# Gated delta rule kernel: the products kept with a minus sign, the inverse's first transposed level copied from SBUF

## The reference, cut to what matters

```python
g = jnp.cumsum(g.reshape(Bq, H, NC, CHUNK), axis=-1)
decay = jnp.where(tril, jnp.exp(g[..., :, None] - g[..., None, :]), 0.0)
M = jnp.where(stril, jnp.einsum('bhncd,bhnmd->bhncm', k_beta, k) * decay, 0.0)
T = jax.scipy.linalg.solve_triangular(eye + M, jnp.broadcast_to(eye, M.shape), lower=True)
v_c = jnp.einsum('bhnij,bhnjd->bhnid', T, v_beta)
k_cumdecay = jnp.einsum('bhnij,bhnjd->bhnid', T, k_beta * jnp.exp(g)[..., None])
```

## Time and profile before

| | |
|---|---|
| median of 3 runs | 1333.41 us (1332.9 to 1334.39) |
| profiled execution, its own time | 1335.4 us |
| its span in the trace | 1333.6 us |
| PE busy | 1217.2 us |
| DVE busy | 1037.8 us |
| ACT busy | 903.4 us |
| POOL busy | 756.3 us |
| granted TensorE clock, mean | 0.985 |

### The profile page before, as it was taken

How to read it: one execution, slowest core, us unless ns; L and a number is a source line. 1 busy time by engine, 2 the same in 40 slices (tenths; PEclk the granted TensorE clock), 3 DMA queues, 4 the chain that set the end, 5 groups by cost and what they waited for, 6 DMA issues and landing times.

```text
span 1333.6 us, 32082 instructions
## 1 busy us (share of the span) xinstructions
PE 1217.2 (91%) x11612; PEld 863.4 (65%) x11612; DVE 1037.8 (78%) x1641; ACT 903.4 (68%) x1715; POOL 756.3 (57%) x792
## 2 busy tenths in 40 slices
PE   3678999999999999999999999999977589999997
PEld 2346676767767676767667676767665356666664
DVE  5586979888797979888897979798865676666565
ACT  2668888888978888888878888888863222222221
POOL 1255666667666766667665766666676667444100
PEclk9999999999999999999999999999999789999999
DMA  3111110101111111101110111100110056445331
GB/s 112 36 57 34 33 38 29 42 25 41 33 58 31 35 34 33 41 26 42 33 57 13 54 33 33 42 26 17 32 35 25 24 168 201 142 146 157 111 103 40
DMA packets 51623, 75.64 MB, mean 57 GB/s; under 512 B 8358, under 2 KB 27208, under 8 KB 51468
## 3 DMA queue, kind: packets, MB, share of 16 engines
q1 hardware_dynamic: 51396, 73.46, 18.0%
q10 hardware_dynamic: 72, 0.14, 0.0%
HBM read 72.26 MB, written 1.32 MB: 55 GB/s over the span
## 4 chain that ended last, share of the span: by engine, by line
PE 73%; DVE 12%; issue 8%; ACT 3%; POOL 2%; DMA 1%; SPq 1%; DVEq 0%; ACTq 0%; POOLq 0%
PE bank L582 15%; PE products L537 9%; PE bank L830 9%; DVE sil L1229 7%; PE products L767 6%; PE products L753 4%; PE products L741 4%; PE products L636 3%; PE bank L665 3%; PE bank L673 3%; PE bank L645 3%; PE bank L601 2%; PE bank L724 2%; PE products L621 2%; PE bank L705 2%
## 5 line engine op out<-in xcount | busy, mean ns | idle before, releaser
L582 PE MATMUL bank<-xT,whl 128*128 128x512 f16 x1152 | 296.6, 384 | 26.8 <-DVE sil L1229 26.7
L1229 DVE SCALAR_TENSOR_TENSOR sil<-bank,cw,sil 128x510 f32<-128x510 f32 (+2 forms) x384 | 283.4, 738 | 16.1 <-ACT sil L919 12.1
L582 PEld LDWEIGHTS bank<-xT,whl 128*128 128x128 f16 x1152 | 98.7, 98 | 125.3 <-DVE sil L1229 38.8
L1110 ACT ACTIVATE kq<-vtok 128x512 f16<-128x512 f32 x94 | 59.1, 630 | 177.1 <-DVE vtok L1499 176.0
L1288 DVE CAST_PREDICATED t<-levm,bank 128x512 f16<-128x512 uint8 x192 | 136.2, 710 | 39.0 <-PE bank L665 36.3
L1499 DVE SCALAR_TENSOR_TENSOR vtok<-products,b1s,zs 128x512 f32<-128x512 f32 x94 | 70.5, 750 | 87.4 <-PE products L537 87.1
L1300 DVE CAST_PREDICATED u<-levm,bank 128x512 f16<-128x512 uint8 x192 | 135.4, 705 | 0.0
L1017 ACT ACTIVATE x<-bank 128x512 f16<-128x512 f32 x160 | 96.2, 601 | 54.1 <-PE bank L645 52.7
L1565 POOL TENSOR_TENSOR hthl<-hz,hthl 128x512 f16<-128x512 f32 x64 | 74.2, 1159 | 93.8 <-ACT hthl L1054 93.8
L1624 POOL TENSOR_TENSOR at<-kqm,ex 128x256 f32<-128x256 f32 x128 | 102.7, 807 | 26.1 <-issue 14.5
L767 PE MATMUL products<-wohl,hthl 128*128 128x256 f16 x768 | 96.8, 277 | 9.3 <-POOL hthl L1565 8.9
(11 more groups left out here) (219 smaller groups left out, 3086.2 us busy)
## 6 DMA issues: line engine op xcount, KB each, us to landing
grow<-rowsc SPq DMA_DIRECT2D x64, 256.0 KB, 3.3
wt<-wqkvz SPq DMA_DIRECT2D x16, 768.0 KB, 4.4
wt<-wm SPq DMA_DIRECT2D x47, 256.0 KB, 2.8
zs<-gsc SPq DMA_DIRECT2D x35, 256.0 KB, 3.4
wo<-wout SPq DMA_DIRECT2D x16, 256.0 KB, 3.2
zs<-gsc SPq DMA_DIRECT2D x16, 224.0 KB, 3.1
zs<-gsc SPq DMA_DIRECT2D x16, 192.0 KB, 3.1
zs<-gsc SPq DMA_DIRECT2D x17, 160.0 KB, 3.3
```

Of the source, the lines that this page charges most:

```text
L582: mm = nc.tensor.matmul(dst[:, :], whl[:, h, k, col:col + HD], xT[:, l, k, half * 512:(half + 1) * 512], start=(k == 0 and m == 0), stop=( ...
L1229: nc.vector.scalar_tensor_tensor(out=dst[:, :, late:S], in0=src[:, :, 0:S - late], scalar=cw[:, q, i, 3 - late:4 - late], in1=dst[:, :, la ...
```

## The change

The strict triangle in the mask constant becomes -1, so `nt`, `n16` and `nl16` hold minus M transposed. Every place that used them changes its sign: level 0's L656 takes the identity, the x evictions lose their factor -1, the first guess is kept with a minus sign and the identity products of `y1` take minus the identity. L658 is left out, since what it wrote into WT_BANK is now what n16 holds; `u(0)` copies it from n16 in SBUF. It no longer waits for w(0) but for the n16 of the pair's second unit. The increment that t(0) waits for stands behind the eight products L656.

```diff
--- before.py
+++ after.py
@@ -141,7 +141,7 @@
-    c32[:, 1] = t < j
+    c32[:, 1] = -1.0 * (t < j)
@@ -653,9 +653,8 @@
                     for m in range(8):
-                        nc.tensor.matmul(X_BANK[:, m * 64:(m + 1) * 64], N[:, m], halves(eye[:], 0)[:, 4, :, 0],
-                                         start=True, stop=True)
-                    mm = nc.tensor.matmul(packed(WT_BANK, 0), eye[:, 4], halves(N, 0)[:, :, :, 1], start=True, stop=True)
+                        mm = nc.tensor.matmul(X_BANK[:, m * 64:(m + 1) * 64], N[:, m], halves(eye[:], 0)[:, 0, :, 0],
+                                              start=True, stop=True)
                     mm.then_inc(s_wlm, 1)
@@ -699,13 +698,13 @@
-                nc.tensor.matmul(R_BANK[:, :], eye[:, 0], guess, start=(c == 0), stop=False, skip_group_check=True)
+                nc.tensor.matmul(R_BANK[:, :], eye[:, 4], guess, start=(c == 0), stop=False, skip_group_check=True)
...
-                nc.tensor.matmul(Y_BANK[:, :], eye[:, 0], guess, start=True, stop=False, skip_group_check=True)
+                nc.tensor.matmul(Y_BANK[:, :], eye[:, 4], guess, start=True, stop=False, skip_group_check=True)
@@ -1014,9 +1013,9 @@
-                    ins = nc.scalar.mul(halves(X, n)[:, :, :, 0], packed(X_BANK, n), -1.0)
+                    ins = nc.scalar.copy(halves(X, n)[:, :, :, 0], packed(X_BANK, n))
                 else:
-                    ins = nc.scalar.mul(X[:, :, 0:64], X_BANK[:, :].rearrange("p (m c) -> p m c", c=64), -1.0)
+                    ins = nc.scalar.copy(X[:, :, 0:64], X_BANK[:, :].rearrange("p (m c) -> p m c", c=64))
@@ -1026,7 +1025,7 @@
-                nc.scalar.copy(y0[:].rearrange("p b v d -> p (b v d)"), Y_BANK[:, :]).then_inc(s_y0, 1)
+                nc.scalar.mul(y0[:].rearrange("p b v d -> p (b v d)"), Y_BANK[:, :], -1.0).then_inc(s_y0, 1)
@@ -1291,8 +1290,12 @@
                 if n == 0:
-                    wait_p(dve, s_wlm, U, 6, 1)
+                    G, b = U
+                    wait_u(dve, s_n16, (G, b + 1), 1, 1)
                     wait_p(dve, s_ut, U, 1, 1)
+                    nc.vector.copy_predicated(halves(Ut, 0)[:, :, :, 1], by4(1, 0), halves(n16[:, turn(U)], 0)[:, :, :, 1]
+                                              ).then_inc(s_uup, 1)
+                    return
```

## The result

The changed kernel takes 1345.53 us (median of 6 runs, 1341.64 to 1349.22) beside 1334.56 us (6 runs, 1332.9 to 1338.49) of the kernel before: a ratio of 1.0078, with a 95% interval of 1.006 to 1.0097. It is slower by 8 to 13 us. The profiled execution took 1342.43 us, one of the quicker ones; 7.0 us of the difference can be looked at in its trace.

The account below looks back on a forecast made before the run. DVE and PE were taken as full together where both inverses start. Second pairs 6.9, first pairs 0.5, ends and late pair 0.6, less 0.3 for ACT gave +7.7 us; from the median 1333.41, forecast 1341.1, range 1329.5 to 1346.

Parts of the forecast that it names:

- case A: The forecast itself: u(0), with two SBUF inputs, loses time to GpSimd; 1341.1 us, own range 1337 to 1346, chance 0.68.
- the sum: Whole kernel: 6.9 for second pairs, 0.5 for first pairs, 0.6 for ends and late pair, less 0.3: +7.7 us.
- B: At u(0), a predicated copy does not share with GpSimd as nt does and stays 0.72 us; 1330.0 us, chance 0.15.
- C: The loss at u(0) is absorbed, or removing L658 frees nothing; 1334 us, no change, chance 0.08.
- D: At u(0), GpSimd's next instruction, L1588, goes first too; 26 us more, 1359.8 us, chance 0.03.
- E: The source makes u(0) about 0.065 us shorter, and it still stalls; 1339.0 us, chance 0.06.
- four pairs at the ends: Pairs at the kernel's two ends, each between −0.2 and +0.45 us; with one late first pair 0.6 us together.
- Part 1: Removing L658 brings t(0) and the PE work behind it 0.22 us earlier in first pairs; alone worth 3.1 us.
- Part 2: u(0) reading n16 from SBUF waits for GpSimd's running instruction; in second pairs 0.47 us lost, 0.46 taken per period.
- In first pairs: u(0) starts at 616.87, loses 0.31 us to L1588 and ends 0.08 later; w(1) comes 0.04 later.
- The cover on GpSimd: GpSimd's next instruction is pushed back by up to 0.6 us, hidden by its idle time of 3.24 or 0.89 us.
- Part 3: On ACT, 192 x evictions become copies and 64 first guesses scaled activations; −0.3 us in all, between −3 and +1.

Follow-up runs that it names:

- v0s_writes_only: Changed kernel with GpSimd's v0s replaced by two zero fills of the same tile, which read no SBUF; 1337.4 us, ratio 1.0014 to the kernel before.
- no_product_psum: Changed kernel without L658 (kept for the very first pair), but u(0) reading whatever the PSUM bank holds; 1336.12 us, ratio 1.0000 to the kernel before.
- after_again: The changed kernel, unchanged, measured again beside the other kernels on the same chip; 1345.21 us, ratio 1.0076 to the kernel before.

## Why the prediction was right, and where it was not

The forecast was 1341.1 against 1333.41, a ratio of 1.0058; measured was 1.0078. The direction, the place and the mechanism of case A are what the trace and the runs show. That the number came this close is in part luck: in the first pairs two errors met, and first and second pairs both lost somewhat more than the sum had, which the start of the profiled execution hid. B falls with v0s_writes_only beside the changed kernel: the same predicated copy is long or short by what its neighbour reads. C falls with the period, D with hsq, which waited for u(0) and not the other way round. E is not borne out: undisturbed, u(0) takes 0.72 us from SBUF, as it did from PSUM. (D's own terms, 26.1 us on 1333.4, give 1359.5 and not 1359.8. The sum's four pairs at the ends are four together with the late one, or they would be 33 pairs.)

*Part 1, L658's worth (14 × 0.22 us): wrong.* I said that t(0) could start at 615.60, since "taps follow each other every 0.65 us". They don't. 0.65 us is the distance from a tap to an instruction that doesn't need it. The second of two taps adds to what the first has written, waits for it in `tap`, and so starts only when it has ended. The row had it: 1.61 us for two taps, less 0.73 for the second, leaves 0.88 between their starts, which makes 615.18 and, with 0.65 more, 615.83 for t(0), to the hundredth. t(0) was waiting for the tap and not for L658. On PE the product did stand in the path of x(1), as the chain had it, but the next projection behind x(1) waits for a tap as well, and w(1) for u(0): the gain lasted for 1 us. no_product_psum says the same in time. Among the signs of being right, "PE 12.4 us less busy" took the records' full 388 ns; records overlap, and PE was 7.5 us less busy.

*Part 2, the loss at u(0) in second pairs (0.46): right.* Forecast 0.47 of loss with 0.59 us of v0s remaining; measured 1.19 against 0.72 with 0.60 remaining (in 14 pairs; I had counted 15, with the first one, where 0.36 us remained and 0.23 were lost). Neither was nt, from which the cost was taken, the instruction that meets GpSimd most: L1505 (`kq<-vtok,kq`, two SBUF inputs too) begins inside a GpSimd instruction with more than 0.13 us to go 36 times of 94, nt 24 times of 64, and it is held in the same way, 1.24 us in the median of these 36 and 0.68 otherwise. *In first pairs* I had u(0) start at 616.87 with 0.31 of loss, ending 0.08 later than before. It did end 0.08 later, from another sum: it did not start earlier, 0.20 us of hsq remained, and 0.08 were lost. Two errors from the one misread row cancelled: that this came out is luck.

*The cover on GpSimd: right.* Its pushed-back instructions cost it 0.46 us each and PE nothing that can be seen: from w(1) to the next w(0), the 29 stretches in the middle of the kernel together are the same as before to 0.1 us. qx and hsq on GpSimd before, then after:

```profile
L1631 POOL TENSOR_TENSOR qx<-cross,exb 128x256 f32<-128x256 f32 x128 | 94.0, 734 | 2.3 <-ACT exb L985 2.3
L1588 POOL TENSOR_TENSOR hsq<-hsq,qsq 128x512 f32<-128x512 f32 x64 | 81.9, 1280 | 38.2 <-ACT hsq L1042 38.1
```

```profile
L1634 POOL TENSOR_TENSOR qx<-cross,exb 128x256 f32<-128x256 f32 x128 | 100.7, 787 | 1.8 <-ACT exb L984 1.8
L1591 POOL TENSOR_TENSOR hsq<-hsq,qsq 128x512 f32<-128x512 f32 x64 | 88.3, 1380 | 38.2 <-ACT hsq L1041 38.1
```

*Part 3, ACT (−0.3 us): too small to be seen in time, so neither shown nor refuted.* An x took 10 ns less, not the 18 of the bound, and a first guess 17 more, beside the earlier trace rows:

```profile
L1016 ACT CAST x<-bank 128x512 f16<-128x512 f32 x160 | 94.6, 591 | 60.3 <-PE bank L645 59.3
...
L1028 ACT ACTIVATE y<-bank 128x512 f16<-128x512 f32 x64 | 38.4, 600 | 32.5 <-PE bank L689 32.5
```

*The sum.* From the first w(0) to the last the profiled kernels differ by 8.3 us (927.9 and 936.2 us, from the start of L656 to that of the last), where the sum had 7.7. In parts: from the first w(0) to the second the changed kernel's execution was 1.1 us quicker (after_again 0.3): from 84 to 90 us its granted clock was 1.00, in the kernel before it was 0.72. The way from w(0) to w(0) of the last two pairs was 0.4 longer. In the 29 pairs between, the loss is 9.0 us (8.5 in after_again): 7.4 between w(0) and w(1) of 15 second pairs (forecast 6.9), 1.5 in 14 first ones, of which 0.4 in the late pair (forecast 0.5 and up to 0.45 for the late one). Each first pair lost 0.08 where the sum had 0.04.

The comparisons say 8 to 13 us. The profiled execution gave 7.0 as its first w(0) came 1.4 us earlier. The changed kernel's other runs lie up to 7 us above its profiled one, those with a lower mean granted clock highest (0.979 at 1349.94 us, 0.989 at 1343.08 among those of after_again). The one of 1349.94 us was profiled, and its trace is 7.5 us longer than that of 1342.43 us, though from the first w(0) to the 31st it took 913.9 us and the other 913.6. The rest is the first w(0), 1.4 us later, the distance of the last two w(0), 25.6 us and not 22.6, and what lies behind, 336.2 us and not 333.3. In that last period PE was busy for 2.55 us of 987 to 992, and from 992 to 997 its granted clock was 0.53, near the lower of the two levels (1.2 GHz); the quicker execution had 2.28 us of 985 to 990, and a clock of 1.00 behind it. So the spread is made at the ends of the kernel and with the clock, and not at u(0) in the periods. Such a fall of the clock ahead of the last w(0) stands in four of the six traces kept with u(0) from SBUF, and in two of the six with it from PSUM. That the change makes it more frequent is not shown.

## What to carry to other kernels

Replacing a PE product and its PSUM bank by a direct copy from SBUF trades a PSUM input for an SBUF one: see whether the instruction that results has any PSUM input left, and if not, look in the timeline for what GpSimd reads at that moment. A loss is about the remainder of that GpSimd instruction, and it matters only if someone stands right behind the copy. Two SBUF inputs are not needed for it. The kernel before had a plain copy with one, beside a GpSimd instruction with one tensor input:

```profile
638.64 0.69 POOL L1552 TENSOR_SCALAR wo<-wo,nw_sb 128x512 f32<-128x512 f32 x1 [0.98 <-DMA wo<-wout]
638.73 0.64 DVE L1250 COPY sc<-scal 128x64 f32<-128x64 f32 x1
```

The shortest of these 16 copies takes 0.17 us; here 0.60 us remained. In the changed kernel's trace, of the instructions that take an input from PSUM, the taps, t, the other levels of u, rr, hz from the products and r1h all stayed under 0.76 us, with GpSimd under way or not. What exactly decides, the number of SBUF inputs, their type or the kind of instruction, no run here was made for.

And before a product is priced as removable, ask what else ends at the same moment: two instructions on one tile can wait for each other without any idle time in the row.

## What the runs showed of the hardware that was not expected

A predicated copy with mask and data in SBUF shares with GpSimd what a product of two tensors shares: with a GpSimd instruction that reads SBUF under way it waits for its end less 0.12 to 0.14 us (remainders of 0.20 to 1.15 us), and then goes ahead of the next one in GpSimd's queue. The forecast had this as its likeliest case. What it did not have is how cleanly it is bound to reading: with 0.40 us of a fill remaining, which only writes, u(0) took 0.72 us, and a fill begun within u(0) took its 0.52. Nor had it the size of the other direction. GpSimd's hsq took 1.74 us in place of 1.28, and 14 us were added to GpSimd's busy time without one instruction more, so a longer mean on GpSimd may be DVE's doing.
